# Routing of a mixture-of-experts layer in three parts instead of two, and the last slot's attention output ahead of the other batch's second FFN matmul

## The reference

```python
x = x + _L0_xcond_ref(_layernorm(x), cond, ctx, ...)   # six layers
x = x + _L0_ffn_ref(_layernorm(x), router_w, router_b, w1, b1, w2, b2)

# _L0_ffn_ref, with T = 2048 tokens, K = 2, E = 8, cap = 640
logits = xf @ router_w + router_b
probs = jax.nn.softmax(logits, axis=-1)
topk_p, topk_i = jax.lax.top_k(probs, K)
...
rank = jnp.arange(A) - starts[se]        # place of a token in its expert's list
keep = rank < cap
slot = jnp.where(keep, se * cap + rank, E * cap)
buf = jnp.zeros((E * cap + 1, d), x.dtype).at[slot].set(xf[st])
...
h = jax.nn.gelu(jnp.einsum('ecd,edf->ecf', buf, w1) + b1[:, None, :])
eo = jnp.einsum('ecf,efd->ecd', h, w2) + b2[:, None, :]
out = jnp.zeros_like(xf).at[st].add(eo_flat[slot] * w)
```

## Time and profile before

| | |
|---|---|
| time, median of 3 runs | 3958.15 us (3956.56 to 3959.05) |
| the profiled execution's own time | 3955.36 us |
| its span | 3953.5 us |
| busy share | PE 94%, DVE 71%, ACT 63%, POOL 28% |
| last slot and its sends | about 3640 to 3754 us |
| experts' program | 3758.4 us to the end |

### The profile page before, as it was taken

One profiled execution on the slowest core, in us unless ns is written; L12 is line 12 of the kernel. 1 busy time (PEld: TensorE's weight loads), 2 busy tenths in 40 slices (PEclk: granted clock), 3 DMA queues, 4 the chain that ended last, 5 costly groups with the idle time before them and its releaser, 6 DMA issues. The chain is left out here.

```text
span 3953.5 us, 53043 instructions
## 1 busy us (share of the span) xinstructions
PE 3715.1 (94%) x19504; PEld 1677.8 (42%) x19504; DVE 2797.2 (71%) x4497; ACT 2504.4 (63%) x4213; POOL 1111.1 (28%) x998
## 2 busy tenths in 40 slices
PE   4999999999999999999999999999999999998568
PEld 1233454433455433345433345533345533344557
DVE  6788766788766688866688866688866688863322
ACT  1677766677765677766677666577666677656123
POOL 2233322233322232322232322233322233311324
PEclk7999999999999999999999999999999999999879
DMA  7566533366533366533365543366544356532145
GB/s 197 119 159 148 129 76 76 83 155 149 134 77 76 79 152 146 135 85 76 76 152 141 137 92 77 76 146 141 134 90 100 83 138 168 129 70 73 44 119 101
DMA packets 282259, 448.74 MB, mean 114 GB/s; under 512 B 50824, under 2 KB 190224, under 8 KB 281488
## 3 DMA queue, kind: packets, MB, share of 16 engines
q1 hardware_dynamic: 237328, 378.51, 40.1%
q0 software_dynamic: 44672, 66.83, 7.4%
HBM read 278.54 MB, written 170.15 MB: 113 GB/s over the span
## 5 line engine op out<-in xcount | busy, mean ns | idle before, releaser
L1197 ACT ACTIVATE prob<-ps 128x512 f32<-128x512 f32 x3072 | 1758.2, 595 | 1017.6 <-PE ps L1120 1008.2
L1380 DVE TENSOR_REDUCE negmax<-ps 128x2 f32<-128x1024 f32 x1536 | 1818.2, 1218 | 230.7 <-PE ps L1147 222.4
L1133 PE MATMUL psv<-prob,v 128*32 128x512 f32 x6144 | 820.1, 606 | 0.7 <-ACT prob L1197 0.7
L1120 PE MATMUL ps<-qstack,kstack 114*128 114x512 bf16 x1536 | 560.7, 386 | 19.9 <-ACT prob L1197 14.7
L1120 PE MATMUL ps<-xin,zrow 114*128 114x512 bf16 x1536 | 561.1, 387 | 8.8 <-ACT prob L1197 4.1
L1120 PEld LDWEIGHTS ps<-qstack,kstack 114*128 114x128 bf16 x1536 | 141.1, 96 | 570.1 <-ACT prob L1197 398.9
L1095 PE MATMUL side<-nT,wf 128*128 128x256 f32 x1480 | 359.5, 386 | 21.8 <-DVE hT L1480 21.8
L1120 PEld LDWEIGHTS ps<-xin,zrow 114*128 114x128 bf16 x1536 | 141.4, 96 | 558.0 <-ACT prob L1197 386.2
L1106 PE MATMUL side<-wf,hT 128*128 128x256 f32 x1456 | 329.3, 379 | 0.0
L1480 DVE TENSOR_SCALAR hT<-side,f1b 128x256 f32<-128x256 f32 x370 | 161.4, 478 | 211.3 <-PE side L1095 210.7
L1095 PEld LDWEIGHTS side<-nT,wf 128*128 128x128 f32 x1480 | 274.8, 191 | 75.4 <-DVE hT L1480 39.2
(11 more groups left out here) (260 smaller groups left out, 3943.2 us busy)
## 6 DMA issues: line engine op xcount, KB each, us to landing
bounce<-parts SPq DMA_DIRECT2D x288, 256.0 KB, 2.5
value_sums<-osum SPq DMA_DIRECT2D x192, 256.0 KB, 6.8
xin<-bounce SPq DMA_DIRECT2D x192, 192.0 KB, 6.0
zrow<-bounce SPq DMA_DIRECT2D x192, 192.0 KB, 6.5
qstack<-bounce SPq DMA_DIRECT2D x192, 192.0 KB, 5.7
kstack<-bounce SPq DMA_DIRECT2D x192, 192.0 KB, 6.3
bounce<-low SPq DMA_DIRECT2D x96, 256.0 KB, 2.1
hT<-value_sums POOLq DMA_DIRECT2D x94, 256.0 KB, 5.1
```

Of the source, the lines that this page charges most:

```text
L1120: nc.tensor.matmul(ps2[:, n % RING2, :], kk[0:ROWS, h, kt * P:(kt + 1) * P], q[0:ROWS, h, :], start=True, stop=True).then_inc(s_p2full, 1)
L1133: mm = nc.tensor.matmul(psv[32 * i:32 * i + 32, 0, :], v[j % 2][:, kt, (HD + 1) * h:(HD + 1) * h + 32], prob[:, 4 * (u % 2) + i, :], start ...
L1197: nc.scalar.activation(prob[:, 4 * (u % 2) + i, :], ps2[:, n % RING2, :], ACT.Exp, scale=HD ** -0.5).then_inc(s_prob, 1)
L1380: nc.vector.tensor_reduce(out_at, ps1[:, 2 * (n % 2):2 * (n % 2) + 2, :], AX, ALU.max, negate=True).then_inc(s_p1free, 1)
```

## The change

The routing of the last slot is cut in two by tiles: part 0 are batches 0 and 1 (`SENT = 2 * TT` tiles), part 1 is batch 2. All route functions take bounds `lo, hi` instead of a count, and work on slices of the same buffers. Part 0 has its shift at place 4, exponentials at 5, pick at 11, tail at 12 and ZR at 13; part 1 at 20, 21, 22, 22 and 23. POOL sends part 0's 16 rows in the last slot. Part 1's goals go to a new small buffer `q.goalu`, and its 8 rows are sent as the first DMAs of the experts' program, ahead of the fourth batch's 8.

In the table `LAST`, O and LT of the last batch move ahead of the other batch's F2: O to places 8 and 9, F2 of the other batch to 10, 11, 13 and 14, LT to 12 between them; F1, F2 and the gelus move up by one or two places, `RECIP` from 7 to 2 and `NORM` from 10 to 5. The third batch's ZT and ZL go from 15 to 17 to 18 and 19.

```diff
 LAST = {
-    "M": [0, 0], "HV": [], "HT": [], "HQ": [], "HK": [], "O": [(12,), (13,)], "LT": [(15,), (15,)],
+    "M": [0, 0], "HV": [], "HT": [], "HQ": [], "HK": [], "O": [(8,), (9,)], "LT": [(12,), (12,)],
...
+SENT = 2 * TT
...
-def route_pick(nc, link, each, r, q, t0, n):
+def route_pick(nc, link, each, r, q, t0, lo, hi):
...
+        goalu = sb("goalu", [P, 2, EARLY - SENT], U32)
...
+        ROUTED = ((0, SENT), (SENT, EARLY))
...
-                for b, at in enumerate((0, 1, 15)):
+                for b, at in enumerate((0, 1, 18)):
                     plan[at] += [(k, "ZT", 2 * b, 0, 1)]
                     plan[at + (b == 1)] += [(k, "ZT", 2 * b + 1, 0, 1)]
-                    plan[at + 1 + (b > 0)] += [(k, "ZL", b, 0, 1)]
-                plan[26].append((k, "ZR", 0, 0, 1))
+                    plan[at + 1 + (b == 1)] += [(k, "ZL", b, 0, 1)]
+                for c, at in enumerate((13, 23)):
+                    plan[at].append((k, "ZR", c, 0, 1))
...
                 pool.wait_ge(s_pad, PAD_DMAS * 16)
                 pool.wait_ge(s_goal, 1)
+                for t in range(SENT):
                     for i in range(2):
-                        send_row(pool, r, q, 0, t, i).then_inc(q.s_sent, 16)
+                        send_row(pool, r["goalu"], q, 0, t, i).then_inc(q.s_sent, 16)
...
-                    if k == JOBS + 1 and at == 12:
+                    if k == JOBS + 1 and at == 15:
                         routing_rstd(2 * TT, EARLY, 2)
-                    if k == JOBS + 1 and at == 23:
-                        routing_exp()
+                    if k == JOBS + 1 and at in (5, 21):
+                        routing_exp(int(at == 21))
...
-                if k == JOBS + 1 and at == 11:
+                if k == JOBS + 1 and at == 14:
                     wait_read(dve, JOBS, "F2", 3)
                     routing_stats(2 * TT, EARLY)
-                if k == JOBS + 1 and at == 15:
+                if k == JOBS + 1 and at == 16:
                     routing_normed(2 * TT, EARLY, 2)
...
+                for c, (shift, pick, tail) in enumerate(((4, 11, 12), (20, 22, 22))):
+                    lo, hi = ROUTED[c]
+                    if k == JOBS + 1 and at == shift:
+                        wait_read(dve, k, "ZL", c + 1)
+                        route_shift(nc, link, r, lo, hi).then_inc(s_rmax, 1)
+                    if k == JOBS + 1 and at == pick:
+                        dve.wait_ge(s_rexp, c + 1)
+                        dve.wait_ge(s_rconst, NE)
+                        dve.wait_ge(s_rsmall, 48)
+                        route_pick(nc, link, each, r, q, 0, lo, hi).then_inc(s_pick, 1)
+                    if k == JOBS + 1 and at == tail:
+                        route_tail(nc, link, r, q, 0, lo, hi)
...
-                    route_goal(nc, link, ranked, r, bank, EARLY).then_inc(s_goal, 1)
+                    goalu = q.goalu[:, :, :] if c else r["goalu"][:, :, 0:SENT]
+                    route_goal(nc, link, ranked, r, bank, goalu, *ROUTED[c]).then_inc(s_goal, 1)
...
         @blk.gpsimd
         def _(pool):
             triangle(pool, r, s_const, 0)
+
+            for t in range(EARLY - SENT):
+                for i in range(2):
+                    send_row(pool, q.goalu, q, SENT, t, i).then_inc(q.s_sent, 16)
             pool.wait_ge(s_goal, 1)
```

More of the change, by code:

```diff
@@ L73 @@
 LAST = {
[3 rows of a table removed]
[L77 to L78 removed]
[3 rows of a table added]
+    "SPLIT": (), "GELU": (18, 22), "PARTS": 0, "RECIP": 2, "NORM": (5, 5),
+    "LN_LT": dict(stats=[9, 9, 9, 9], aggregate=9, guess=9, newton=10, tiles=[10, 10, 10, 10]),
 }
@@ L182, in route_pick @@
+def route_pick(nc, link, each, r, q, t0, lo, hi):
+    n = hi - lo
+    pr, top, idx, idxf = (r[name][:, lo:hi, :] for name in ("pr", "top", "idx", "idxf"))
+    mx, inv = r["mx"][:, lo:hi], r["lnv"][:, lo:hi]
+    link(nc.vector.tensor_reduce(mx, pr, AX, ALU.add))
+    link(nc.vector.reciprocal(inv, mx))
+    link(nc.vector.tensor_tensor(pr, pr, inv[:, :, None].to_broadcast([P, n, NE]), ALU.mult))
     each(lambda t: nc.vector.max(top[:, t, :], pr[:, t, :]), n)
     each(lambda t: nc.vector.max_index(idx[:, t, :], top[:, t, :], pr[:, t, :]), n)
-    link(nc.vector.tensor_copy(idxf[:, :, :], idx[:, :, 0:2]))
+    link(nc.vector.tensor_copy(idxf, idx[:, :, 0:2]))
+    pick = r["pick"][:, :, lo:hi, :]
@@ new lines, in route_pick, with route_tail @@
+    return nc.vector.tensor_tensor(q.pickb[:, t0 + lo:t0 + hi, :], pick[:, 0, :, :], pick[:, 1, :, :], ALU.add)
+def route_tail(nc, link, r, q, t0, lo, hi):
+    mx, inv, top = r["mx"][:, lo:hi], r["lnv"][:, lo:hi], r["top"][:, lo:hi, :]
+    token = q.token[:, t0 + lo:t0 + hi]
+    tail = lambda c, w: q.zrow[:, t0 + lo:t0 + hi, D + c:D + c + w]
+    link(nc.vector.tensor_copy(tail(0, 1).rearrange("p t c -> p (t c)").bitcast(U32), token))
+    for i in range(2):
+        link(nc.vector.tensor_scalar(r["spare"][:, i, lo:hi], token, float(NE * CAP + i * T), None, ALU.add))
+    link(nc.vector.tensor_tensor(mx, top[:, :, 0], top[:, :, 1], ALU.add))
+    link(nc.vector.tensor_scalar(mx, mx, 1e-9, None, ALU.max))
+    link(nc.vector.reciprocal(inv, mx))
+    link(nc.vector.tensor_copy(tail(1, 1), r["idxf"][:, lo:hi, 0:1]))
+    link(nc.vector.tensor_tensor(tail(2, 2), top[:, :, 0:2], inv[:, :, None].to_broadcast([P, hi - lo, 2]), ALU.mult))
@@ L215, in route_ranks, with route_goal @@
     return mm
-def route_goal(nc, link, ranked, r, bank, n):
-    pick, at, kept, goal, spare = (r[name] for name in ("pick", "at", "kept", "goal", "spare"))
+def route_goal(nc, link, ranked, r, bank, goalu, lo, hi):
+    n = hi - lo
+    pick = r["pick"][:, :, lo:hi, :]
+    at, kept, goal, spare = (r[name][:, :, lo:hi] for name in ("at", "kept", "goal", "spare"))
     rank = bank[:, 0:n * NE].rearrange("p (t e) -> p t e", e=NE)
```

89 lines of the change are left out of this document (32 added, 57 removed), and 4 rows, old and new, of the table LAST.

## The result

| | before | after |
|---|---|---|
| median | 3958.60 us (3956.56 to 3959.35, 4 runs) | 3929.38 us (3926.95 to 3930.94, 4 runs) |
| profiled span | 3953.5 us | 3927.2 us |

The ratio is 0.9926, 95% interval 0.9909 to 0.9944: 29 us faster, where 40.5 were forecast. 3929.38 lies above the range (3911.5 to 3925).

The account below looks back on a forecast made before the run. POOL's sends of routed rows were taken to set the end of the layers' program, 33.5 us after everybody else. The sum 7.5 (PE) + 33.5 - 0.5 = 40.5 us gave a median of 3917.6 us, range 3911.5 to 3925.

Parts of the forecast that it names:

- The 33 us behind the slot: End of the layers' program: POOL's tail of sends, 33.5 us after everybody else, shrinks to 0.5 us.
- rival 1: Change of programs: it costs 4.58 us whoever is last, giving 3921.7 us; chance 0.12.
- the 4.58 us: Last send's end to the next program's first POOL instruction: mostly POOL finishing its transfers; 0.5 us taken when DVE is last.
- rival 5: Sends beside DVE's work: each takes longer than 1.273 us, break-even at 3.7, 3970 us at 4.2; chance 0.02.
- The term of 7.5 us: Last slot: reordering brings DVE's last addition from 3724.97 to 3717.4, 7.5 us earlier.
- The waits of 5.42 and 4.00 us: PE's waits in the last slot for the last batch's norm and the routing norm; the reordering was to remove them.
- Hidden: DVE's reciprocal at place 2 waits about 1.5 us for the sums' load, while F1's fourth chunk isn't ready anyway.
- 10 us to spare: Last slot: sixteen sends and POOL's finish end at 3707.3, under PE's work that lasts to 3717.4.
- Rival 3: Last slot gets no shorter, as routing's DVE work delays F1's and F2's reads; 3925.1 us, chance 0.06.
- 7.2 us to spare: Experts' start: eight early sends leave POOL free at 10.9 us, its next send is due at 18.07.
- Rival 2: Experts' program: DVE waits behind the early sends, 4 to 7.7 us, giving 3921.5 to 3925; chance 0.08.
- rival 4: Change of programs: PE's clock doesn't fall to 0.50, up to 4 us gained, 3913.6 us; chance 0.05.

Follow-up runs that it names:

- e1: Changed kernel with POOL, behind its 16 sends in the last slot, also waiting for the read of the last F2 chunk; median 3934.1 us.
- e2: Changed kernel with the last slot's 16 sends moved to the start of the experts' program, 24 early sends there; median 3935.8 us.
- e7: Changed kernel with the slot's 16 sends as plain POOL DMAs of the same bytes to spare rows, output wrong; median 3918.4 us.
- e3: Changed kernel with the reciprocals at place 3 instead of 2, behind the read of F1's fourth chunk; median 3930.7 us.
- e5: Changed kernel with 12 sends in the slot, only after F1's last chunk is read, and 12 early in the experts' program; median 3923.1 us.
- e9: Changed kernel with 12 sends in the slot, each waiting for a chunk's read, and 12 early in the experts' program; median 3921.6 us.
- e12: Changed kernel with a dummy POOL memset of 512 columns and a wait between the slot's 16 sends; median 3923.3 us.
- e13: Changed kernel with a dummy POOL memset of 256 columns and a wait between the slot's 16 sends; median 3922.9 us.
- e10: Changed kernel with the slot's 16 indirect sends writing neighbouring spare rows in order, output wrong; median 3929.3 us.
- e8: Changed kernel with the slot's 16 sends as plain DMAs issued from SP's queue to spare rows, output wrong; median 3919.9 us.

## Why the prediction was wrong, and where right

- **The 33 us behind the slot: right.** The change of programs is 0.70 us from the last addition's start (0.33 of DVE's idling), so rival 1 is out. The reason was half known: I took the 4.58 us for POOL finishing its transfers, and e1 shows 4.14 of them 25 us after the last one went out. Here POOL's finish is over at 3707.4, and 22 us of slot hide it.
- **Sends beside DVE's work stay at 1.27: right**, 1.28 on the mean in the slot, and the longest of the sixteen is busy for 1.07 us; rival 5 and the factor of five of the Trainium skill, SBUF — State Buffer, section "A bandwidth-pool intuition that's wrong", are not seen.
- **Two collisions of the pick with POOL's additions, 1.0 us:** seen, L187 and a cast, less than 1 us in all.
- **The order's gain in PE's slot: nearly right.** Without late signals the slot is 74.42 (e2) to 75.49, forecast 73.4. The term of 7.5 us was 1.1 to 2.1 us too large. The waits of 5.42 and 4.00 us are gone.
- **"Hidden", of DVE's wait for the load: wrong by little.** The wait was 2.88 us, not 1.5, and 3 us at partly half clock came behind it (0.99 us and no such dip in e7, whose code is the same up to there); in e3, without it, the slot is only 0.4 us shorter.
- **The step that failed** is the first of the change: "The cover is the rest of the slot, to 3717.4 (below): 10 us to spare." I asked whether the sends fit under the slot, and whether DVE slows them; not what they do to the others. The sum has no term for it, which puts it at nothing. They do fit, but not for nothing: 16 indirect sends back to back make PE's signals late and cost the slot 12.0 us (87.11 against e7's 75.12). Aligned at the slot's first chunk, PE is 0.5 us behind e7 before the transposes, 9.6 behind at F1's sixth chunk, where the signal was late, and 12.0 at the first F2 chunk, behind the half clock. Two signs named beforehand failed with it: "no wait of PE over 2 us in the last slot" (5.97 us) and a granted clock near 1.00 in all of it (0.56).
- **Rival 3** (the slot gets no shorter, 3925.1) had the direction and not the cause: it laid the loss on DVE's work in front of the reads, and stopped at zero gain; the slot is 6.25 us longer.
- **Eight early sends hidden: right** (18.06). "7.2 us to spare" is **wrong**: four more already cost 2.2 to 2.5 us. Rival 2 is out for eight, and real for twelve, by another mechanism.
- **Clock at the experts' start 0.50: right**, rival 4 is out (third window).
- The rest, what follows the experts' start: 1.7 us longer than before in the changed kernel, with 0.4 to 1.8 in the runs with 8 early sends; that spread is not explained.

What stays open: why the indirect form does it. The trace shows that PE's work ends on time (by its modelled ends, and PE goes on to its next chunk) and that its signals act late, in batches (F1's chunk and the logits behind it reached DVE within 1.6 us, though PE had ended them 2.8 apart), PE's first and after some twelve sends DVE's own; it does not show what they queue behind. Nor is there a run without a profiler's recording, so that recording may have a part in it isn't excluded: of the 512 increments of `s_sent` the trace of the kernel before has all, that of the changed kernel 276.

The runs with spaced sends are the fastest here with a right output, with e5 (3923.1 us) beside them: e9, e12 and e13 have medians of 3921.6 to 3923.3 us, ratios to before 0.9904 to 0.9906 (0.989 to 0.992), against 3929.4 and 0.9926. That they beat the kernel before is clear. Against the changed kernel the intervals overlap; the single runs of e13 (3918.2 to 3924.0) and of the changed kernel (3927.0 to 3930.9) do not, though these two didn't run side by side. e10, whose sends are those of the changed kernel, ran beside e9: 3929.3 against 3921.6.

## What to carry to other kernels

When work is hidden under another engine's, ask not only whether it fits and whether it is slowed, but what it slows: in the trace of the change, look for idle readers that start later than 0.04 us after the end of the chunk they wait for. Indirect DMAs of GpSimd beside a dense stretch of PE should be held apart, with a wait between them (here 1.46 us instead of 1.27 was enough), or stand where no later chunk wants the late bank back, as in e5. And a block's end behind GpSimd's DMAs cost about 4 us here, unless GpSimd came to it early.

## What the runs showed of the hardware that I had not expected

- Indirect DMAs of GpSimd (128 rows of 1,040 B) back to back at 1.27 us beside dense PE work delayed PE's signals by up to 8 us (7.98 in e10), beside F1 from about the seventh on; in e5, beside F2, a signal was still on time with eight out. Plain ones of the same bytes at 0.55 us did not.
- In the experts' program the same rate stretched DVE's waits for itself from 0.03 to as much as 1.2 us a step (e2), from about the twelfth send, and DVE idled up to 10.5 us for a signal of PE.
- At a block's end POOL's finish kept DVE idle for 4.14 us with POOL's last send 25 us back (e1; DRAIN 3.66 us, and 2.35 where POOL had sent nothing in the slot, e2 and e8).
- A memset of GpSimd on 512 columns lengthened DVE's instructions beside it, from 0.41 to as much as 0.81 us (e12).
